# Residuals of the attention blocks and of the FFN: from transposes on TensorE to additions on VectorE

## The reference

```
self:   xa  = layernorm(x + mha(x, windows of 8x8), g_self, b_self)       # 64 strips of 8 rows
low:    xl  = layernorm(avgpool4(xa) + mha(avgpool4(xa)), g_self, b_self) # 16x16 pixels an image
cross:  q   = layernorm(xa + mha(q=xa, kv=8x8 windows of xl, stride 2), g_cross, b_cross)
ffn:    o   = layernorm(q + relu(q @ w1 + b1) @ w2 + b2, g_out, b_out)
conv:   y   = batchnorm(conv3x3(sign(o), sign(weight)));  out = o + y
mha(q, kv) = softmax(q wq (kv wk)^T / 4) (kv wv) wf + bf                  # 8 heads of 16
```

## Time and profile before

| what | value |
|---|---|
| median of 3 runs | 2183.79 us (2181.91 to 2187.62) |
| profiled execution, own time | 2176.89 us |
| its span, first to last instruction | 2175.1 us |
| busy: PE / DVE / ACT / POOL | 1997.8 / 1577.2 / 1364.9 / 1247.3 us |
| mean granted TensorE clock | 0.979 of full speed |
| share of the 16 DMA engines, busiest queue | 60.0% |
| moved by DMA | 393.56 MB |

### The profile page before, as it was taken

How to read it: one execution, slowest core, us unless ns; L and a number is a source line. 1 busy time by engine, 2 the same in 40 slices (tenths; PEclk the granted TensorE clock), 3 DMA queues, 4 the chain that set the end, 5 groups by cost and what they waited for, 6 DMA issues and landing times.

```text
span 2175.1 us, 93188 instructions
## 1 busy us (share of the span) xinstructions
PE 1997.8 (92%) x39504; PEld 1604.3 (74%) x39504; DVE 1577.2 (73%) x5093; ACT 1364.9 (63%) x2531; POOL 1247.3 (57%) x1280
## 2 busy tenths in 40 slices
PE   6998889999899999999999998999999999999950
PEld 4886777887788877888778886888778877677730
DVE  3997867777677777787777777777767776666545
ACT  3765656666566665666666665666656666566545
POOL 4665656666566655665566665666556665555410
PEclk9999999999999999999999999999999999999985
DMA  6877755665566655666556656666656664555539
GB/s 178 231 220 199 218 157 166 193 188 151 169 184 181 188 171 164 180 182 185 156 175 197 178 151 179 181 179 192 172 163 179 176 192 129 145 148 148 181 102 410
DMA packets 335053, 393.56 MB, mean 181 GB/s; under 512 B 39984, under 2 KB 239408, under 8 KB 334640
## 3 DMA queue, kind: packets, MB, share of 16 engines
q1 hardware_dynamic: 333792, 386.61, 60.0%
q10 hardware_dynamic: 848, 0.99, 0.1%
HBM read 208.29 MB, written 160.27 MB: 169 GB/s over the span
## 4 chain that ended last, share of the span: by engine, by line
PE 81%; DVE 7%; ACT 4%; DMA 3%; issue 3%; POOL 2%; SPq 0%; POOLq 0%; DVEq 0%; ACTq 0%
PE ps_hid L702 11%; PE ps_y L714 10%; PE ps_o L650 9%; PE ps_proj L565 9%; PE ps_s L631 7%; PE ps_hid L733 6%; PE ps_y L682 5%; PE ps_s L637 5%; PE ps_max L621 5%; PE ps_y L669 4%; PE ps_proj L590 3%; PE ps_t L690 2%; PE ps_t L663 2%; PE ps_t L722 1%; DVE negmax L927 1%
## 5 line engine op out<-in xcount | busy, mean ns | idle before, releaser
L1086 POOL TENSOR_TENSOR prob_lo<-prob,prob_hi 128x512 f16<-128x512 f32 x528 | 611.5, 1158 | 641.1 <-ACT prob_hi L800 640.9
L927 DVE TENSOR_REDUCE negmax<-ps_max 128x8 bf16<-128x512 f32 x528 | 359.4, 681 | 195.1 <-PE ps_max L621 190.2
L799 ACT ACTIVATE prob<-ps_s 128x512 f32<-128x512 f32 x528 | 314.3, 595 | 204.7 <-PE ps_s L637 195.3
L939 DVE TENSOR_TENSOR onorm<-ps_o,rden 64x128 f32<-64x128 f32 x1056 | 304.8, 289 | 25.5
L800 ACT ACTIVATE prob_hi<-ps_s 128x512 f16<-128x512 f32 x528 | 312.6, 592 | 0.0
L838 ACT ACTIVATE hid<-ps_hid,columns_sb 128x512 f32<-128x512 f32 x256 | 176.0, 688 | 209.5 <-PE ps_y L714 116.5
L650 PE MATMUL ps_o<-vb,prob_hi 128*128 128x68 f16 x4224 | 288.9, 195 | 7.5 <-POOL prob_lo L1086 3.8
L631 PEld LDWEIGHTS ps_s<-qs,ks 64*64 64x64 f16 x8448 | 174.1, 109 | 147.1 <-issue 117.9
L702 PE MATMUL ps_hid<-xf,w_sb 128*128 128x512 f32 x512 | 275.5, 620 | 3.3 <-ACT yconv L857 2.2
L650 PEld LDWEIGHTS ps_o<-vb,prob_hi 128*128 128x128 f16 x4224 | 229.1, 98 | 43.0 <-issue 18.8
L714 PE MATMUL ps_y<-w_sb,hid 128*128 128x128 f32 x2048 | 252.5, 275 | 0.0
(11 more groups left out here) (112 smaller groups left out, 3419.4 us busy)
## 6 DMA issues: line engine op xcount, KB each, us to landing
k_rows<-k_flat SPq DMA_DIRECT2D x256, 256.0 KB, 3.2
qs<-q_rows SPq DMA_DIRECT2D x512, 128.0 KB, 3.2
ks<-k_rows SPq DMA_DIRECT2D x128, 512.0 KB, 4.4
q_rows<-q_flat SPq DMA_DIRECT2D x128, 256.0 KB, 2.4
vb<-v_flat SPq DMA_DIRECT2D x128, 136.0 KB, 3.3
vb<-values_out SPq DMA_DIRECT2D x128, 136.0 KB, 3.3
xin<-in_x SPq DMA_DIRECT2D x64, 256.0 KB, 4.5
self_out<-xa SPq DMA_DIRECT2D x64, 256.0 KB, 3.1
```

The lines of the kernel that those rows point to most:

```text
L799: activation(prob[:, pair_no(u, k) % 2, :], ps_s[:, :], ACT.Exp)
L927: v.tensor_reduce(negmax[:, pair_no(u, k) % 2, :], ps_max[:, :].rearrange("p (a t) -> p a t", t=TOK), AX.X, ALU.max, negate=True).then_inc ...
L939: done = v.tensor_tensor(onorm[r, u.seq % 2, k, :].rearrange("p (w j d) -> p j w d", w=2, j=4), blocks[r, :, :, DH * h2:DH * h2 + DH], r2[ ...
L1086: g.tensor_tensor(prob_lo[:, i, :], prob[:, i, :], prob_hi[:, i, :], ALU.subtract).then_inc(s_prob, 1)
```

## The change: what it does

**Residuals.** The 512 transposes of `attention_residual` for self and cross units and the 256 of `ffn_residual` are gone; the low units keep theirs (16, as `low_residual`). Instead the tokens are held by token: `xtok` is loaded from a second copy of the input (`x_tokens`) for a self unit and from `self_tokens` for a cross unit. DVE adds `ps_y` and `xtok` into `ysum` (stage `add`, 128 times) and `ps_y2` and `ctok` into `ysum2` (stage `add2`, 64 times), each 128x512 in fp32. Statistics and `xn` are then read from `ysum` and `ysum2` in SBUF, not from PSUM. `ps_y` is free after `add`; it was free after `apply`.

**Scale and shift by token.** POOL no longer adds the bias to `xin` and `xf`. It adds the bias to `xtok` of self units (stage `token_bias`, 64 times) and computes `xn` times gain plus shift with rows broadcast over tokens (stage `gain`, 128 times two instructions), into `stok` (stored to `self_tokens`) or `ctok` (read by `add2`). The shifts have the next bias folded in. `xn` has two buffers.

**Loads.** 192 DMAs of 256 KB are added (128 loads of `xtok`, 64 stores of `stok`). `xin` has 3 buffers for 4, and a buffer is free after the last projection.

**Start.** TensorE waits for `wq`, `wk`, `wv` and `consts` alone, which are issued first. The other loads go out on ACT's queue behind them; the signs of the convolution's weights are taken in ACT's first `turned` stage; the memsets of two of the `vb` tiles go to DVE, and `v_flat` is POOL's first.

**Order.** All offsets are new, and `LOW_AFTER` is 20 for 17. All three queues that carry the new work have it between old stages. In the fences below the line numbers are those of each program.

```diff
-RING = 4
+RING = 3
+TRING = 2
 LAG = 15
-LOW_AFTER = 17
+LOW_AFTER = 20
...
-CROSS = dict(load=-10.84, q_put=-8.03, k_put=-7.53, q=-7.49, k_take=-6.97, q_hi=-6.85, q_move=-6.39, q_lo=-6.21,
-             v_fetch=-5.99, k_move=-5.72, bias=-4.22, turn=4.36, turned=4.68, resid=5.52, stats=5.59, project=5.64,
...
+CROSS = dict(load=-10.05, q=-7.68, q_put=-7.45, q_hi=-7.45, q_lo=-6.93, k_take=-6.6, k_put=-5.48, q_move=-4.24,
+             k_move=-3.54, v_fetch=-1.39, load_tokens=0.49, turn=4.39, turned=4.78, add=5.5, stats=5.51, project=5.59,
...
-PAIR = dict(rough=-2.02, exp=-1.22, scores=-1.03, prob_lo=-0.81, weigh=0.02)
+PAIR = dict(rough=-1.99, exp=-1.2, scores=-1.11, prob_lo=-0.31, weigh=0.2)
...
+        first_loads = [(wk_sb[:, :, :], wk.rearrange("m c n -> c m n")), (wv_sb[:, :, :], wv.rearrange("m c n -> c m n")),
+                       (consts_sb[:, :], consts)]
+        setup_loads = [(columns_sb[:, :], columns), (rows_of(rows_sb[:, :, :]), rows)]
         setup_loads += [(wf_sb[64 * h2:64 * h2 + 64, :, :], wf[h2].rearrange("m r n -> r m n")) for h2 in range(2)]
...
+            sp.dma_start(wq_sb[:, :, :], wq.rearrange("m c n -> c m n")).then_inc(s_first, 16)
...
+                    sp.wait_ge(s_proj, last_project(in_slot[u.seq]))
...
+            def load_tokens(u):
+                if in_token_slot[u.seq] is not None:
+                    sp.wait_ge(s_add, add_no["add", in_token_slot[u.seq].seq, None])
+                if u.kind == "self":
+                    src = x_tokens[u.no, :, :]
+                else:
+                    sp.wait_ge(s_tokens_stored, 16 * u.no + 16)
+                    src = self_tokens[u.no, :, :]
+                sp.dma_start(xtok[:, token_slot[u.seq], :], src).then_inc(s_xtok[token_slot[u.seq]], 16)
+
+            def store_tokens(u):
+                sp.wait_ge(s_gain, gain_no["gain", u.seq, None])
+                sp.dma_start(self_tokens[u.no, :, :], stok[:, :]).then_inc(s_tokens_stored, 16)
...
+            def y_free(u):
+                p = before_y[u.seq]
+                if p is not None and p.kind == "low":
+                    pe.wait_ge(s_xn, xn_done[p.seq])
+                elif p is not None:
+                    pe.wait_ge(s_add, add_no["add", p.seq, None])
...
-            def attention_residual(u):
-                if before_resid[u.seq] is not None:
-                    pe.wait_ge(s_xn, xn_done[before_resid[u.seq].seq])
-                pe.wait_ge(s_plus, plus_no["bias", u.seq, None])
-                residual(ps_y, u.pairs, tokens_of(u)).then_inc(s_resid, 1)
...
             def project_out(u):
+                low = u.kind == "low"
+                if not low:
+                    y_free(u)
                 pe.wait_ge(s_t_taken, turn_no["turn", u.seq, None])
                 for p in range(u.pairs):
                     done = mm(ps_y[:, C * p:C * p + C], oT[:, C * p:C * p + C], wf_sb[:, which(u), :],
-                              start=False, stop=True, skip_group_check=True)
+                              start=not low, stop=True, skip_group_check=True)
                 done.then_inc(s_y, 1)
...
-            def ffn_residual(u):
-                if u.no:
-                    pe.wait_ge(s_xn2, PAIRS * u.no)
-                pe.wait_ge(s_plus2, u.no + 1)
-                residual(ps_y2, PAIRS, xf_plus).then_inc(s_resid2, 1)
-
             def ffn_out_part(u, b):
+                if b == 0 and u.no:
+                    pe.wait_ge(s_add2, u.no)
                 pe.wait_ge(s_hid_taken, hid_no[f"h{b}", u.seq, None])
                 for p in range(PAIRS):
                     done = mm(ps_y2[:, C * p:C * p + C], hid[:, b % 2, C * p:C * p + C], w2_sb[:, b, :],
-                              start=False, stop=(b == FB - 1), skip_group_check=True)
+                              start=(b == 0 and p == 0), stop=(b == FB - 1), skip_group_check=True)
...
+            pe.wait_ge(s_first, 16 * len(first_loads) + 16)
...
+            def signs():
+                act.wait_ge(s_setup, 16 * len(setup_loads))
+                cw = convs[:, :, :].rearrange("p a b -> p (a b)")
+                activation(cw[:, 0:1024], rows_of(xf[:, :, :])[:, 0:1024], ACT.Sign)
+                activation(cw[:, 1024:TAPS * C], rows_of(hid[:, :, :])[:, 0:TAPS * C - 1024], ACT.Sign
+                           ).then_inc(s_prep_a, 1)
+                act.wait_ge(s_prep_a, 1)
+                act.wait_ge(s_prep_g, 5)
...
+            def add_residual(u):
+                dve.wait_ge(s_y, y_no["project", u.seq, None])
+                if u.kind == "self":
+                    dve.wait_ge(s_token_plus, u.no + 1)
+                else:
+                    dve.wait_ge(s_xtok[token_slot[u.seq]], 16 * token_loads[u.seq])
+                if apply_no[u.seq]:
+                    dve.wait_ge(s_xn, xn_done[u.seq] - u.pairs)
+                v.tensor_tensor(ysum[:, :], ps_y[:, :], xtok[:, token_slot[u.seq], :], ALU.add).then_inc(s_add, 1)
+
             def stats_of(u):
                 n = y_no["project", u.seq, None]
-                dve.wait_ge(s_y, n)
+                if u.kind == "low":
+                    dve.wait_ge(s_y, n)
+                else:
+                    dve.wait_ge(s_add, add_no["add", u.seq, None])
+                y = ps_y if u.kind == "low" else ysum
...
-                    v.tensor_scalar(xn[:, C * p:C * p + C], ps_y[:, C * p:C * p + C], mv[:, p, 0:1],
+                    v.tensor_scalar(xn[:, n % 2, C * p:C * p + C], y[:, C * p:C * p + C], mv[:, p, 0:1],
...
+            def add_residual2(u):
+                dve.wait_ge(s_f, FB * u.no + FB)
+                dve.wait_ge(s_gain, gain_no["gain", u.seq, None])
+                if u.no:
+                    dve.wait_ge(s_xn2, PAIRS * u.no)
+                v.tensor_tensor(ysum2[:, :], ps_y2[:, :], ctok[:, :], ALU.add).then_inc(s_add2, 1)
+
             def stats2_of(u):
-                dve.wait_ge(s_f, FB * u.no + FB)
+                dve.wait_ge(s_add2, u.no + 1)
...
+            def add_token_bias(u):
+                pool.wait_ge(s_xtok[token_slot[u.seq]], 16 * token_loads[u.seq])
+                t = by_pair(xtok[:, token_slot[u.seq], :])
+                g.tensor_tensor(t, t, row(0), ALU.add).then_inc(s_token_plus, 1)
+
+            def gain_by_token(u):
+                n, m = gain_no["gain", u.seq, None], which(u)
+                pool.wait_ge(s_xn, xn_done[u.seq])
+                if u.kind == "self":
+                    to = by_pair(stok[:, :])
+                    if u.no:
+                        pool.wait_ge(s_tokens_stored, 16 * u.no)
+                else:
+                    to = by_pair(ctok[:, :])
+                    if u.no:
+                        pool.wait_ge(s_add2, u.no)
+                g.tensor_tensor(to, by_pair(xn[:, apply_no[u.seq] % 2, :]), row(1 + 2 * m), ALU.mult
+                                ).then_inc(s_gain0, 1)
+                pool.wait_ge(s_gain0, n)
+                g.tensor_tensor(to, to, row(2 + 2 * m), ALU.add).then_inc(s_gain, 1)
 
```

More of the change, by code:

```diff
@@ L59 @@
[L59 to L63, removed]
+SELF = dict(load=-10.79, q=-7.67, q_hi=-7.48, q_lo=-7.16, k_lo=-6.67, k=-6.53, k_hi=-6.39, q_put=-6.13, v_hi=-5.48,
+            v=-5.28, k_put=-5.13, v_lo=-5.02, q_move=-4.7, k_move=-3.81, v_move=-2.69, load_tokens=-1.03,
+            token_bias=1.51, turned=3.92, turn=4.06, project=5.12, add=5.19, stats=5.87, rstd=6.62, apply=6.87,
+            spread_out=6.95, spread=7.36, pool=7.44, gain=7.79, store=9, store_tokens=9.99)
@@ L111, in stages_in_order, with attention_conv @@
     return [r[1:] for r in row]
-def attention_conv(nc, x, wq, wk, wv, wf, columns, w1, w2, convw, consts, out):
+def attention_conv(nc, x, x_tokens, wq, wk, wv, wf, columns, rows, w1, w2, convw, consts, out):
     units = units_in_order()
@@ L149, in attention_conv @@
             last["v"] = u
-    before_turn, before_spread, before_resid = {}, {}, {}
-    for stage, u, what in order:
-        for name, of in (("turn", before_turn), ("spread", before_spread), ("resid", before_resid)):
-            if stage == name:
-                of[u.seq] = last.get(name)
-                last[name] = u
     xn_done = {}
@@ L161, in attention_conv @@
     plus_no = numbered("bias")
+    add_no = numbered("add")
+    gain_no = numbered("gain")
+    before_apply, apply_no = {}, {}
+    for stage, u, what in order:
+        if stage == "apply":
+            apply_no[u.seq] = len(apply_no)
+            before_apply[apply_no[u.seq]] = u
+    before_y = {}
+    for stage, u, what in order:
+        if stage == "project":
+            before_y[u.seq] = last.get("y")
+            last["y"] = u
+    token_slot, in_token_slot, token_loads = {}, {}, {}
+    for u in units:
+        if u.kind != "low":
+            token_slot[u.seq] = len(token_slot) % TRING
+            in_token_slot[u.seq] = last.get(("t", token_slot[u.seq]))
+            last["t", token_slot[u.seq]] = u
+            token_loads[u.seq] = (len(token_slot) - 1) // TRING + 1
     same_b = {}
```

(4 more changed lines are left out.)

164 lines of the change are left out of this document (91 added, 73 removed).

## The result

The changed kernel is slower: 2334.5 us (median of 4 runs, 2327.1 to 2335.9) against 2185.5 us (4 runs, 2181.9 to 2187.6), ratio 1.068 with a 95% interval of 1.065 to 1.071. The forecast was 2103 us with a range from 2066 to 2160. The median of before lies 8.6 us above the profiled execution from which the sum was made.

The account below looks back on a forecast made before the run. TensorE, busy 92%, was taken as the bound until the last 66 us. 2175.1 us of span - 80 (transposes) - 5.8 (start) + 12 (additions) = 2101.3, with 1.8 around it 2103 us; range 2066 to 2160.

Parts of the forecast that it names:

- Statistics and `xn` from SBUF: VectorE reading sums from SBUF: costed at nothing; by an estimate of 67 ns less each, new waits about +5, not +12.
- Rival 4: VectorE's `xn` from SBUF holds GpSimd up, so `prob_lo` takes longer: +60 us, 2163 us; chance 5%.
- Transposes, -80 us: 192 groups of four leave TensorE: at most 84.5 us at 0.44 each, 76.5 by the chain's share; middle taken.
- Additions, +12 us: 192 additions on VectorE at 0.691 us make TensorE wait: half of a +25 us growth, bounds -10 to +132.7.
- Start, -5.8 us: TensorE and ACT begin earlier, 7.1 us at ACT, less 1.3 for the signs; between -7.4 and 0.
- GpSimd, 0: Bias additions go, `token_bias` and `gain` come, net +68.6 us of GpSimd work; `prob_lo` not late, at worst +40 us.
- Rival 2: `gain` on GpSimd makes `prob_lo` late for TensorE: +40 us, 2143 us; chance 12%.
- Wait for `ps_y`, 0: `project` on TensorE waits for the `add` of the unit before, about 8 us ahead: no cost.
- DMAs, 0: 192 added issues on SP and later moves of `qs` and `ks`: median covered, so 0; at worst +32 us.
- rival 3: `qs` and `ks` arrive late before TensorE's rough scores: +32 us, 2135 us; chance 8%.
- rival 5: Stops for `qs` and `ks` vanish with the new order and no addition is late: 2067 us; chance 10%.
- Rival 1: VectorE becomes the bound and the kernel slower, 2224 us if all 192 additions show; chance 5%.

Follow-up runs that it names:

- experiment 2: The changed kernel with both sums written in place in PSUM, where statistics and `xn` read them; nothing left out. 2164.2 us, ratio 0.990.
- experiment 1: The kernel before the change, with `xn` and `xn2` computed from a constant tile in SBUF, not from PSUM. 2206.6 us, ratio 1.010.
- experiment 7: The changed kernel with both sums in PSUM and VectorE's additions cut to 8 columns. 2128.9 us, ratio 0.974.
- experiment 6: The changed kernel with both sums in PSUM and GpSimd's `token_bias` and `gain` cut to 8 columns. 2160.4 us, ratio 0.990.
- experiments 7 to 9: 7 as above; 8: changed kernel, sums in PSUM, offsets of the kernel before, 2192.6 us; 9: kernel before without the 192 transpose groups, 2145.2 us.
- experiments 2 or 11: 2 as above; 11: changed kernel, `xn` reads its sum in SBUF and `rstd` copied into PSUM, nothing left out. 2157.4 us, ratio 0.988.

## Why the prediction was wrong

*The step that failed: "Statistics and `xn` from SBUF … I cost it at nothing."* It cost 170 us (2334.5 against 2164.2 in experiment 2). The text said that no row had it "for contiguous columns" and stopped at an estimate of a gain. The free duration did fall (404 to some 335 ns, about the 67 ns of the estimate), but the instruction is held while GpSimd works. Rows of the kernel before showed this for smaller instructions that go from SBUF to SBUF, in minimum, median, maximum:

```profile
L1004 DVE TENSOR_SCALAR xlow<-low_sum x16: 214/230/683, 150.8 to 1788.3; 128x128 f32<-128x128 f32 x16
```
```profile
L1026 DVE COPY kvpad<-kvpad x8: 209/210/1103, 198.9 to 1853.2; 128x96 f32<-128x96 f32 x8
```

A maximum of three and of five times the median, within an instruction that had already begun, was the warning; I had not looked at it. The Trainium skill (SBUF — State Buffer, "Who interferes with whom") has the rule: a VectorE instruction in a mode with two ports contends with GpSimd, one with two inputs in SBUF contends with GpSimd instructions that read SBUF, and whichever is issued first has the shared ports for its whole length while the other is blocked. The runs agree in the forms tried: `tensor_scalar` from SBUF held (740 ns), two tensors in SBUF held (764 ns), one of them in PSUM not (343 ns), statistics not (281 ns). That the hold lasts the other's whole length is not borne out beside GpSimd's bias additions in experiment 1, where 28 holds end half way.

The two profiled executions lie 176 us apart. Of these, 88 are in TensorE's busy time (2044.1 against 1955.7 us for the same 38736 matmuls) at a granted clock of 0.950 against 0.975, and 87 in its idle time (288.7 against 201.4). The clock was low early in the kernels in which the attention block's `xn` was held, and rose once it was not. Why is not shown: from 40 to 200 us TensorE was idle for 26.4 us at 0.83 and for 23.8 us at 0.97, and no run changed the clock alone.

*Rival 4* named the two engines and the place, and had the mechanism the wrong way round: VectorE is held by GpSimd, whose `prob_lo` stayed at a mean of 1164 ns. It was priced at +60 with 5%; its sign, a longer `prob_lo`, did not come.

*Transposes, -80 us.* Measured 40. The chain's pieces of 0.44 us were taken as what goes when they go. TensorE's busy time fell by 0.29 us a group, probably since the group overlapped with its neighbours at both ends, and new waits took 25 us of that: it seems that TensorE was so close to the others that it caught up with them. The chain's share was an upper bound here, and the lower end, 76.5, was none.

*Additions, +12 us.* Their duration, 684 and 691 ns, was right. Their cost is 35 us by experiment 7, inside the bounds of -10 to +132.7, and above even the full growth of +25 that I had halved. TensorE's waits for VectorE, 50 us by the forecast, sum to 55 in experiment 2 and to 149 in the changed kernel.

*Start, -5.8 us.* TensorE began at 6.23 us (5.7 forecast, 13.10 before), and ACT took its first projection at 8.34 us (8.2 forecast, 15.27 before). No run has the start alone.

```profile
6.23 2.07 PE L616 MATMUL ps_proj<-xin,wq_sb 128*128 128x256 f32 x4 [6.23 <-DMA consts_sb<-in_consts]
```

*GpSimd, 0.* The durations were 1272 ns and not 1158 (407 us, not 371), and the cost in experiment 6 is 3.8 us, not told from nothing and by the intervals no more than some 12. Rival 2 fell, though its sign came: the waits for `prob_lo` rose to 39.5 us, from 3.8 before. They are 35.0 us in experiment 2 and 30.7 in experiment 6, with GpSimd's new work cut, so that this work is not what raised them, and what did is open. *Wait for `ps_y`, 0; DMAs, 0:* no stop of TensorE for `xtok` or `ps_y` shows, and rival 3 had the wrong sign: the new order brought the stops for `qs` and `ks` down, from 18.4 us to 5.9 in experiment 2, and is worth 28 us, part of what rival 5 held. *Rival 1* did not come by the additions, though its sign did (waits for VectorE over 100 us), and VectorE came to 34% of the chain, by the held `xn`.

The miss is 231.5 us: 170.3 for `xn`, 39.8 for the transposes, 23.3 for the additions, 8.6 for the base of the sum (profiled execution for median), less 10.5, since order, start and the rest brought 16.3 us in place of 5.8. This adds up costs from different kernels as if they were independent, and the last term is what is left over. Open is the rest: by experiments 7 to 9, before - 40 + 35 is 2180.5, and with the old order the run gave 2192.6, some 12 us more though it has the new start too. `gain`, the added transfers and the waits in it are not told apart.

## What to carry to other kernels

Before an operand moves from PSUM to SBUF, look at what GpSimd does at that time. Where GpSimd works much of the time, an fp32 `tensor_scalar` or `scalar_tensor_tensor` of VectorE whose tensors are all in SBUF costs up to one GpSimd instruction more; one tensor input kept in PSUM avoided it here. Look at minimum, median and maximum of similar instructions rather than at a mean: here the warning was in rows of 8 and 16 instructions. And what is taken off the busiest engine can bring less than its fall in busy time, and much less than its share of the chain: 40 us here, for 56 and 76.5. Repaired by experiments 2 or 11, the change brings 1.0 to 1.2%.
